# First group of a fused cross-attention and FFN kernel, rebuilt: load order, Wq centred first, angle sums on GpSimd, real part of four tiles before the imaginary part

## The chip, the cores and the metric

One core of one Trainium2 chip runs the whole program. The metric is the time of an execution on the device in microseconds (us). The core's engines are TensorE (PE in the profile, PEld for its weight loads), VectorE (DVE), ScalarE (ACT), GpSimd (POOL) and SyncE (SP), which issues nearly all transfers. They run side by side and meet only at semaphores.

## The reference

```python
x = x + xattn(layernorm(x), ctx_1024, mask, Wq, bq, Wk, bk, Wv, bv, Wo, bo)   # x: (2, 2048, 512), ctx: (2, 77, 512)
#   Q = q @ Wq + bq; K = ctx @ Wk + bk; V = ctx @ Wv + bv        one head, 77 keys
#   softmax(where(mask, Q K^T / sqrt(512), -1e9)) V @ Wo + bo
h = layernorm(x)
real = h @ cos(theta + theta_noise)                              # theta, phi: (512, 512)
imag = h @ sin(phi + phi_noise)
x = x + sqrt(real * real + imag * imag)
```

## The kernel before

The 4096 rows of x are cut into eight groups of 512 rows, four tiles of 128 rows each; groups alternate between the two batches. Each engine has its own program, written out by hand in the order in which it is to run, and semaphores join them.

**Prepared once.** K is made from the context and Wk, then `A = Wq K^T` (one 512 x 154 matrix for both batches), so that the scores of a group are `x^T` chunks times `A`, and a row `c = bq K^T`. A is centred over its rows (the layer norm's mean is taken out that way): ScalarE copies A to `a_raw`, TensorE multiplies it with `ones_mean`, VectorE subtracts. V times Wo gives `vw`, 77 rows for each batch. The angle matrices come in halves of 128 x 1024. For each half: the sum with the noise (`sum_angle`; theta on VectorE, phi on GpSimd), `turns_of` on ScalarE (two passes that round to whole turns), `reduce_angle` on VectorE (lines 714, 717, 720), `sine` on ScalarE (lines 566, 568: the sine and its fp16 high part `w_hi`), and `low_half_of_sine` on VectorE (line 726: the rest, `w_lo`, counted by `w_ready`: 2 is all of cos, 4 is all of sin).

**Each group.** `scores` on TensorE; `softmax_shift` on VectorE, `exps` on ScalarE, `softmax_total` on VectorE; `attend` on TensorE; `residual` on VectorE (line 793, with the statistics of the second layer norm, 796 and 803); `rstd_of_x2` on GpSimd (341 to 348); `high_half` on ScalarE (591, 596) and `low_half` on VectorE (807), which split the normed rows into two fp16 halves; a DMA transposition of each tile (`transpose_h`, SP line 256); `feed(n, j, part)`, twelve fp16 matmuls of 512 columns for tile j and part 0 (real) or 1 (imaginary); `square` on ScalarE, `add_squares` on VectorE, `roots`, `finish` and the store.

**The first group (0)** attends in fp32 with `vw` itself. All later groups use `vw` scaled by its largest entry and split into fp16 halves, stacked in `vw_stack`. The largest entry is found so: `key_max` on VectorE, a transposition on TensorE, `vw_max` on VectorE, a matmul that spreads it over the partitions, four small VectorE operations up to `vw_scale`; then ScalarE scales and rounds (`vw_hi_ready`), the low half is taken (`vw_lo_ready`), SP stacks both by three transfers. Only with these, and with the probabilities of group 1 split (`high_probs`, `low_probs`) and transposed by a DMA (`transpose_probs(1)`), can `attend(1, 1, 0)` run.

TensorE's program from the first `feed` on: eight feeds of group 0, with the four `attend(1, 1, j)` and `scores(2, 0)` between them, then `step(1)`, whose first is `feed(1, 0, 0)`, up to `step(6)` and the last group. `x_loaded[b]` counts the loads of a batch's x buffer `xb[b]`, `stats_of_x(b, blk)` waits for it; `load_x(0, 1)` brings the rows of group 2 into the buffer that group 0 used.

## Time and profile before

| | |
|---|---|
| time, median of 3 runs | 267.83 us (267.27 to 268.71) |
| span of the profiled execution, first to last instruction | 265.4 us |
| time of the profiled execution itself | not given; 267.8 - 265.4 = 2.4 us lie around the span |
| TensorE busy | 240.6 us (91%) |
| VectorE, ScalarE, GpSimd busy | 183.0, 148.8, 65.7 us |
| matmuls of the first group start | 50.0 us |
| matmuls of the second group start | 86.4 us |
| mean granted clock of TensorE | 0.976 |

An engine's busy share is a mean over the whole run. The run has two stages with different limits: up to 86.4 us the preparation and the first group, in which every engine waits for others at some places, and from there a steady stage. The change is in the first.

### The profile page before, as it was taken

Reading aid. Unit: us, or ns where it says so; the run is one execution under the profiler, and the core shown is the slowest. Engines: PE = TensorE matmul, PEld = TensorE weight load, DVE = VectorE, ACT = ScalarE, POOL = GpSimd, SP = SyncE. Lnnn points to the kernel's source line nnn. Section 1 sums busy time; section 2 is a strip of 40 time slices with the busy share of each in tenths; the row PEclk is TensorE's granted clock in tenths of the full one; section 3 lists DMA queues with packets and bytes.
Section 4 is the critical chain, followed back from the end, with each engine's and each line's share of the span. In section 5 each row is a group of like instructions: output and inputs, shape, how many; then the busy total and the mean of one; then the engine's idle time right before and its main releaser. Section 6 shows DMA issues by size and latency. Waiting matters only on the chain.

```text
span 265.4 us, 3879 instructions
## 1 busy us (share of the span) xinstructions
PE 240.6 (91%) x1223; PEld 132.0 (50%) x1223; DVE 183.0 (69%) x348; ACT 148.8 (56%) x203; POOL 65.7 (25%) x158
## 2 busy tenths in 40 slices
PE   0989779859966999999999999999999999999991
PEld 0899334524722444744474456445644654444440
DVE  2038799995886787778787777786768662964442
ACT  0248477655705792676378447745773577266341
POOL 1000646571334203310430233024203310132000
PEclk9999958999979999999999999999999999999998
DMA  6999930458122895396359736862695244324531
GB/s 210 388 424 411 416 127 0 63 187 229 42 45 40 189 220 227 61 252 206 161 99 244 270 90 169 175 277 59 187 211 235 42 80 79 161 40 79 198 116 46
DMA packets 47948, 44.79 MB, mean 169 GB/s; under 512 B 42454, under 2 KB 42454, under 8 KB 44605
## 3 DMA queue, kind: packets, MB, share of 16 engines
q1 hardware_dynamic: 47269, 44.42, 55.5%
q10 hardware_dynamic: 664, 0.18, 0.3%
q8 instruction: 8, 0.13, 0.2%
q14 instruction: 7, 0.06, 0.1%
HBM read 25.66 MB, written 8.39 MB: 128 GB/s over the span
## 4 chain that ended last, share of the span: by engine, by line
PE 72%; DVE 14%; DMA 4%; POOL 4%; issue 3%; ACT 2%; SPq 0%; DVEq 0%; POOLq 0%; ACTq 0%
PE re L445 10%; PE re L446 10%; PE re L447 10%; PE im L445 9%; PE im L446 9%; PE im L447 9%; PE score_bank L416 7%; DVE angle_w L714 2%; PE att L432 2%; PE att L434 2%; DVE angle_w L717 2%; DMA wk<-in_Wk 2%; DVE stats L735 2%; DVE x L793 1%; DVE stats L796 1%
## 5 line engine op out<-in xcount | busy, mean ns | idle before, releaser
L445 PE MATMUL re<-w_hi,hT 128*128 128x512 f16 x128 | 49.0, 383 | 4.2 <-DMA hT<-h_split 4.2
L591 ACT ACTIVATE h<-x,shift,rstd 128x512 f32<-128x512 f32 x32 | 26.0, 813 | 42.9 <-POOL shift L348 42.9
L445 PE MATMUL im<-w_hi,hT 128*128 128x512 f16 x128 | 48.5, 379 | 0.8 <-DVE w_lo L726 0.8
L446 PE MATMUL re<-w_lo,hT 128*128 128x512 f16 x128 | 49.0, 383 | 0.0
L447 PE MATMUL re<-w_hi,hT 128*128 128x512 f16 x128 | 48.9, 382 | 0.0
L447 PE MATMUL im<-w_hi,hT 128*128 128x512 f16 x128 | 48.5, 379 | 0.0
L446 PE MATMUL im<-w_lo,hT 128*128 128x512 f16 x128 | 48.5, 379 | 0.0
L807 DVE SCALAR_TENSOR_TENSOR h_split<-h,h_split 128x512 f16<-128x512 f32 x32 | 22.0, 689 | 21.2 <-ACT h_split L596 21.2
L416 PEld LDWEIGHTS score_bank<-a_keys,xTb 128*128 128x128 f32 x256 | 29.8, 192 | 1.3 <-issue 0.5
L341 POOL TENSOR_TENSOR veps<-mv,eps 128x1 f32<-128x1 f32 x32 | 11.6, 362 | 73.4 <-DVE mv L803 73.4
L416 PE MATMUL score_bank<-a_keys,xTb 128*128 128x77 f32 x256 | 29.5, 274 | 0.0
L334 POOL TENSOR_TENSOR veps<-mv,eps 128x4 f32<-128x4 f32 x8 | 4.5, 557 | 95.9 <-DVE mv L741 95.9
L602 ACT ACTIVATE sq_re<-re 128x512 f32<-128x512 f32 x32 | 18.6, 583 | 15.2 <-PE re L447 10.3
L824 DVE TENSOR_TENSOR wv<-x,wk 128x2048 f32<-128x2048 f32 x7 | 16.0, 2292 | 15.0 <-ACT wk L607 12.3
L816 DVE TENSOR_TENSOR wk<-sq_re,sq_im 128x512 f32<-128x512 f32 x32 | 21.9, 684 | 5.3 <-ACT sq_im L602 3.8
L793 DVE SCALAR_TENSOR_TENSOR x<-att,inv_total,xb 128x512 f32<-128x512 f32 x32 | 23.6, 736 | 2.1 <-PE att L434 1.9
L602 ACT ACTIVATE sq_im<-im 128x512 f32<-128x512 f32 x32 | 18.8, 588 | 10.1 <-PE im L447 10.1
L796 DVE BATCH_NORM_STATS2 stats<-x 128x6 f32<-128x512 f32 x32 | 22.2, 694 | 1.1
L445 PEld LDWEIGHTS re<-w_hi,hT 128*128 128x128 f16 x128 | 12.7, 99 | 20.6 <-ACT sq_re L602 2.6
L596 ACT ACTIVATE h_split<-h 128x512 f16<-128x512 f32 x32 | 20.2, 632 | 1.5
L445 PEld LDWEIGHTS im<-w_hi,hT 128*128 128x128 f16 x128 | 12.7, 100 | 15.3 <-DVE w_lo L726 0.8
L447 PEld LDWEIGHTS re<-w_hi,hT 128*128 128x128 f16 x128 | 12.6, 98 | 15.5 <-issue 0.6
(115 smaller groups left out, 333.6 us busy)
## 6 DMA issues: line engine op xcount, KB each, us to landing
xTb<-in_xT SPq DMA_DIRECT2D x8, 1024.0 KB, 5.0
xb<-in_x SPq DMA_DIRECT2D x8, 1024.0 KB, 5.5
out_rows<-wv SPq DMA_DIRECT2D x7, 1024.0 KB, 3.9
wk<-in_Wk SPq DMA_DIRECT2D x2, 512.0 KB, 5.3
wqT<-in_WqT SPq DMA_DIRECT2D x1, 1024.0 KB, 8.3
angle_w<-in_theta SPq DMA_DIRECT2D x2, 512.0 KB, 10.2
angle_n<-in_theta_noise SPq DMA_DIRECT2D x2, 512.0 KB, 10.9
wv<-in_Wv SPq DMA_DIRECT2D x1, 1024.0 KB, 13.5
```

The source lines that it names most:

```text
L416: last = nc.tensor.matmul(score_bank[:, KEYS * j:KEYS * j + KEYS], xTb[:, k, P * j:P * j + P], a_keys[:, k, KEYS * batch:KEYS * batch + KEYS],
L445: nc.tensor.matmul(bank_[:, :], hT[j][:, 0, k, :], w_hi[part][:, k, :], start=(k == 0), stop=False)
L446: nc.tensor.matmul(bank_[:, :], hT[j][:, 0, k, :], w_lo[part][:, k, :], start=False, stop=False)
L447: last = nc.tensor.matmul(bank_[:, :], hT[j][:, 1, k, :], w_hi[part][:, k, :], start=False, stop=(k == CH - 1))
L591: nc.scalar.activation(h[j % 2][:, :], x2[b][:, j, :], ACT.Identity, bias=shift2[:, j:j + 1], scale=rstd2[:, j:j + 1]).then_inc(h_made, 1)
L596: nc.scalar.activation(h_split[j][:, 0, :], h[j % 2][:, :], ACT.Copy, scale=H_SCALE).then_inc(hi_made, 1)
L602: nc.scalar.activation((sq_re, sq_im)[part][j % 2][:, :], (re_bank, im_bank)[part][j % 2][:, :], ACT.Square, scale=UNSCALE).then_inc((re_s ...
L793: nc.vector.scalar_tensor_tensor(out=x2[b][:, j, :], in0=att_bank[j % 2][:, :], scalar=inv_total[:, j:j + 1], in1=xb[b][:, j, :], op0=ALU. ...
L796: nc.vector.bn_stats(stats2[:, j, :], x2[b][:, j, :]).then_inc(stats2_made, 1)
L807: nc.vector.scalar_tensor_tensor(out=h_split[j][:, 1, :], in0=h[j % 2][:, :], scalar=H_SCALE, in1=h_split[j][:, 0, :], op0=ALU.mult, op1=A ...
L816: nc.vector.tensor_tensor(power[:, j, :], sq_re[j % 2][:, :], sq_im[j % 2][:, :], ALU.add).then_inc(power_made, 1)
L824: nc.vector.tensor_tensor(result[:, :, :], x2[b][:, :, :], power[:, :, :], ALU.add).then_inc(result_made, 1)
```

## The change

1. **Loads.** `WqT` comes in four chunks, then `xT` and `x` of group 0, `Wv`, the first half of theta, `Wo`, the other half, phi. Before: `WqT` whole, theta, `Wv`, `xT`, `x`, `Wo`, phi. The load of group 1's x goes behind the first two transpositions, and `load_x(0, 1)` from before the third transposition to behind `transpose_probs(1)`.
2. **A.** VectorE centres the rows of Wq itself, chunk by chunk (`bn_stats`, `bn_aggr`, subtract), before the product; `a_raw`, `a_mid` and the mean matmul go; `a_keys` is made from PSUM by VectorE with scale and mask in one pass.
3. **TensorE.** Eleven matmuls on zeros at the very start; `scores(0, 0)` ahead of the V products; the real part of four tiles, then the imaginary part of four tiles, each tile with a PSUM bank of its own (`feed_first`); `scores(2, 0)` goes behind the attends.
4. **Angles.** All four sums on GpSimd; the quarter turn of the cosine is put into the bias of ScalarE's sine, with the absolute value taken by a bitwise VectorE pass instead of the clamp. `sine(1, 1)` stands behind the scaling of `vw`.
5. **`vw`.** `key_max` takes the absolute value itself; ScalarE makes the high half in one pass; the low half goes from GpSimd to VectorE, behind `low_half_of_sine(1, 1)`.
6. ScalarE loads the exp table at the start and the sine table by a dummy; `step(1)` and `step(2)` of ScalarE and steps 1 to 4 of VectorE are written out instead of looped.

```diff
             for half in range(2):
                 chunks = slice(CH // 2 * half, CH // 2 * half + CH // 2)
                 sp.dma_start(wk[:, chunks, :], Wk[:, chunks, :]).then_inc(ld_wk[half], 16)
-            sp.dma_start(wqT[:, :, :], WqT).then_inc(ld_wq, 16)
-            load_angles(0, 0)
-            load_angles(0, 1)
-            sp.dma_start(wv[:, :, :], Wv).then_inc(ld_wv, 16)
+            for k in range(CH):
+                sp.dma_start(wqT[:, k, :], WqT[:, k, :]).then_inc(ld_wq[k], 16)
             load_xT(0, 0)
             load_x(0, 0)
+            sp.dma_start(wv[:, :, :], Wv).then_inc(ld_wv, 16)
+            load_angles(0, 0)
             sp.dma_start(wo[:, :, :], Wo).then_inc(ld_wo, 16)
+            load_angles(0, 1)
             load_angles(1, 0)
             load_angles(1, 1)
-            load_x(1, 0)
...
             transpose_h(0, [0, 1])
-            sp.wait_ge(x2_made, TILES)
-            load_x(0, 1)
+            load_x(1, 0)
             transpose_h(0, [2])
...
             transpose_probs(1)
+            sp.wait_ge(x2_made, TILES)
+            load_x(0, 1)
             transpose_h(1, [0, 1])
...
             rstd_of_x(0)
-            sum_angle(0)
-            sum_angle(1)
-            for j in range(TILES):
-                rstd_of_x2(0, j)
+            sum_angle(0, 0)
+            sum_angle(0, 1)
+            sum_angle(1, 0)
+            rstd_of_x2(0, 0)
+            rstd_of_x2(0, 1)
+            sum_angle(1, 1)
+            rstd_of_x2(0, 2)
+            rstd_of_x2(0, 3)
             rstd_of_x(1)
-            pool.wait_ge(vw_hi_ready, 1)
-            nc.gpsimd.tensor_tensor(vw_lo[:, :, :], vw_scaled[:, :, :], vw_stack[0][0:KEYS, :, :],
-                                    ALU.subtract).then_inc(vw_lo_ready, 1)
...
+            pe.wait_ge(warm_made, 1)
+            for _ in range(WARM):
+                nc.tensor.matmul(prep[7][:, :], warm[:, 0:P], warm[:, :], start=True, stop=True)
...
+            pe.wait_ge(vw_ready, 2)
             pe.wait_ge(w_ready, 2)
-            feed(0, 0, 0)
-            feed(0, 1, 0)
+            feed_first(0, 0)
+            feed_first(1, 0)
+            feed_first(2, 0)
 
             pe.wait_ge(key_max_made, 1)
             nc.tensor.transpose(pT_bank[0:1, 0:KEYS], key_max[:, :], ident[0:KEYS, 0:KEYS]).then_inc(key_max_mm, 1)
+            feed_first(3, 0)
             pe.wait_ge(vw_max_made, 1)
             nc.tensor.matmul(pT_bank[:, P:P + 1], ones_row[:, :], vw_max[:, :], start=True, stop=True).then_inc(vw_max_mm, 1)
             pe.wait_ge(w_ready, 4)
-            feed(0, 0, 1)
-            feed(0, 1, 1)
-            feed(0, 2, 0)
-            feed(0, 2, 1)
-            scores(2, 0)
+            feed_first(0, 1)
+            feed_first(1, 1)
             pe.wait_ge(vw_stacked, 3 * 16)
             attend(1, 1, 0)
-            feed(0, 3, 0)
             attend(1, 1, 1)
+            feed_first(2, 1)
             attend(1, 1, 2)
-            feed(0, 3, 1)
             attend(1, 1, 3)
+            scores(2, 0)
+            feed_first(3, 1)
...
             exps(0)
+            turns_of(0, 0)
             act.wait_ge(pT_mm, 1)
             nc.scalar.activation(probsT[:, :], pT_bank[0:KEYS, :], ACT.Copy).then_inc(pT_copied, 1)
+            nc.scalar.activation(act_scratch[:, 1:2], zero[:, :], ACT.Sin)
+            act.wait_ge(half_pi_made, 1)
+            sine(0, 0)
+            turns_of(0, 1)
+            high_half(0, 0, 0)
+            high_half(0, 0, 1)
+            sine(0, 1)
             turns_of(1, 0)
...
+            high_half(0, 0, 2)
+            high_half(0, 0, 3)
+            sine(1, 0)
             turns_of(1, 1)
+            square_first(0, 0)
+            square_first(1, 0)
+            act.wait_ge(vw_scale_made, 2)
+            nc.scalar.activation(vw_stack[0][0:KEYS, :, :], vw[:, :, :], ACT.Copy,
+                                 scale=vw_scale[0:KEYS, 0:1]).then_inc(vw_hi_ready, 1)
             sine(1, 1)
+            square_first(2, 0)
+            square_first(3, 0)
             exps(1)
             high_probs(1)
+            square_first(0, 1)
+            square_first(1, 1)
...
+            for k in range(CH):
+                dve.wait_ge(ld_wq[k], 16)
+                nc.vector.bn_stats(wq_stats[:, k, :], wqT[:, k, :]).then_inc(wq_stats_made, 1)
+                dve.wait_ge(wq_stats_made, k + 1)
+                nc.vector.bn_aggr(wq_mean[:, k, :], wq_stats[:, k, :]).then_inc(wq_mean_made, 1)
+                dve.wait_ge(wq_mean_made, k + 1)
+                nc.vector.tensor_scalar(wqT[:, k, :], wqT[:, k, :], wq_mean[:, k, 0:1], None,
+                                        ALU.subtract).then_inc(wq_centred, 1)
```

VectorE's order after the keys (each name is a function above; `values_ready(b)` adds `bo` to `vw`):

```
softmax_shift(0), softmax_total(0), reduce_angle(0,0), values_ready(0), residual(0,0), residual(0,1),
low_half_of_sine(0,0), reduce_angle(0,1), low_half(0,0), residual(0,2), low_half(0,1), values_ready(1),
residual(0,3), low_half_of_sine(0,1), reduce_angle(1,0), key_max, low_half(0,2), low_half(0,3),
low_half_of_sine(1,0), reduce_angle(1,1), vw_max, stats_of_x(1,0), vw_scale, softmax_shift(1),
low_half_of_sine(1,1), vw_lo, low_probs(1), softmax_total(1), add_squares(0,0), stats_of_x(0,1),
mean_of_x(2), residual(1,0), add_squares(0,1), residual(1,1), low_half(1,0), ...
```

## Rows read from the trace of the kernel before

**Rows 1.** The page: GB/s in the 40 slices of 6.6 us.

```profile
GB/s 210 388 424 411 416 127 0 63 187 229 42 45 40 189 220 227 61 252 206 161 99 244 270 90 169 175 277 59 187 211 235 42 80 79 161 40 79 198 116 46
```

**Rows 2.** Windows: stretch, its length, busy us by engine, granted clock, DMA.

```profile
73.50:75.50 2.00, 0.00 (x1) 0.00 (x0) 2.00 (x5) 0.00 (x0) 0.00 (x0) 0.97 0.69 134
75.50:78.70 3.20, 3.12 (x8) 1.17 (x9) 2.95 (x9) 0.00 (x0) 1.51 (x3) 0.50 0.00 0
...
86.30:265.40 179.10, 173.32 (x880) 88.41 (x880) 122.95 (x242) 104.73 (x144) 34.92 (x111) 0.99 0.55 154
```

**Rows 3.** Timeline of TensorE: start us, us, engine line op out<-in [idle before <-releaser].

```profile
49.99 0.38 PE L445 MATMUL re<-w_hi,hT 128*128 128x512 f16 x1 [0.72 <-DMA hT<-h_split]
...
69.81 3.69 PE L416 MATMUL score_bank<-a_keys,xTb 128*128 128x77 f32 x32
75.58 0.59 PE L432 MATMUL att<-vw_stack,pT 128*128 128x512 f16 x1 [2.07 <-issue]
...
86.36 0.39 PE L445 MATMUL re<-w_hi,hT 128*128 128x512 f16 x1 [2.14 <-DMA hT<-h_split]
```

**Rows 4.** Loads: SyncE's and VectorE's timeline, DMA issues (us to landing).

```profile
6.31 0.50 SPq L243 DMA_DIRECT2D wo<-in_Wo  x1
...
15.92 1.23 DVE L704 SCALAR_TENSOR_TENSOR angle_w<-angle_w,angle_n 128x1024 f32<-128x1024 f32 x1 [1.33 <-DMA angle_n<-in_theta_noise]
...
wo<-in_Wo SPq DMA_DIRECT2D x1, 1024.0 KB, 20.5
```

**Rows 5.** Timeline from the statistics of x to the first softmax.

```profile
28.15 0.38 DVE L741 BATCH_NORM_AGGREGATE mv<-stats 128x2 f32<-128x6 f32 x4
28.61 1.28 POOL L334 TENSOR_TENSOR veps<-mv,eps 128x4 f32<-128x4 f32 x1 [26.77 <-DVE mv L741]
...
31.12 0.92 DVE L751 SCALAR_TENSOR_TENSOR logits<-score_bank,rstd,c_keys 128x77 f32<-128x77 f32 x4 [1.29 <-POOL rstd L336]
```

**Rows 6.** Timeline of GpSimd's angle sums and VectorE beside them.

```profile
30.97 4.89 POOL L328 TENSOR_TENSOR angle_w<-angle_w,angle_n 128x1024 f32<-128x1024 f32 x2
...
32.58 1.07 DVE L760 TENSOR_TENSOR shifted<-logits,top 128x308 f32<-128x308 f32 x1
...
34.18 2.76 DVE L714 SCALAR_TENSOR_TENSOR angle_w<-turns,angle_w 128x1024 f32<-128x1024 f32 x1
...
90.11 0.48 DVE L760 TENSOR_TENSOR shifted<-logits,top 128x308 f32<-128x308 f32 x1
```

**Rows 7.** Groups by line, 0 to 75 us: busy us, mean ns, idle before.

```profile
L735 DVE BATCH_NORM_STATS2 stats<-xb 128x6 f32<-128x512 f32 x11 | 6.8, 680 | 0.0
...
L717 DVE SCALAR_TENSOR_TENSOR angle_w<-turns,angle_w 128x1024 f32<-128x1024 f32 x4 | 4.9, 1228 | 0.1
...
L726 DVE SCALAR_TENSOR_TENSOR w_lo<-angle_n,w_hi 128x1024 f16<-128x1024 f32 x4 | 4.8, 1210 | 0.1
...
L793 DVE SCALAR_TENSOR_TENSOR x<-att,inv_total,xb 128x512 f32<-128x512 f32 x4 | 3.0, 746 | 0.1
...
L720 DVE TENSOR_SCALAR angle_w<-angle_w 128x1024 f32<-128x1024 f32 x4 | 2.8, 694 | 0.1
```

**Rows 8.** Timeline: tile 3 of group 0, from its statistics to ScalarE.

```profile
55.10 0.18 DVE L803 BATCH_NORM_AGGREGATE mv<-stats 128x2 f32<-128x6 f32 x1
...
60.37 0.81 ACT L591 ACTIVATE h<-x,shift,rstd 128x512 f32<-128x512 f32 x1 [2.71 <-POOL shift L348]
```

**Rows 9.** Timeline of ScalarE: a table load and what follows it.

```profile
25.13 1.28 ACT L566 ACT_TABLE_LOAD   x1
...
26.43 1.06 ACT L566 ACTIVATE angle_n<-angle_w 128x1024 f32<-128x1024 f32 x1
```

**Rows 10.** SyncE's timeline and DMA issues of short windows (us to landing).

```profile
72.33 1.27 SPq L263 DMA_TRANSPOSE pT<-p_split  x1
...
hT<-h_split SPq DMA_TRANSPOSE x1, 3.1
...
xb<-in_x SPq DMA_DIRECT2D x1, 1024.0 KB, 5.8
```

More of the change, by code:

```diff
@@ L401, in _ @@
             last.then_inc(c_mm, 1)
-            pe.wait_ge(a_copied, CH)
-            for k in range(CH):
-                last = nc.tensor.matmul(prep[1][:, 0:KK], ones_mean[:, :], a_raw[:, k, :],
-                                        start=(k == 0), stop=(k == CH - 1))
-            last.then_inc(mean_mm, 1)
             def scores(m, batch):
@@ L480, in _ @@
             attend_first(1)
[L481 removed]
+            project_values(1, range(1, CH))
             attend_first(2)
@@ L607, in roots @@
                 nc.scalar.activation(power[:, :, :], power[:, :, :], ACT.Sqrt).then_inc(root_made, 1)
[L609 to L613 removed]
             act.wait_ge(ld_bv, 16)
             for c in range(CH):
[L616 removed]
+                bank_ = prep[2 + c] if c < 2 else prep[4 + c]
                 act.wait_ge(vT_mm, c + 1)
```

246 lines of the change are left out of this document (132 added, 114 removed).

## The prediction

> **What bounds the kernel now.** I read the slices and windows first. From 86.3 us on TensorE is busy 173.3 of 179.1 us, the rest being the tail in which the last group is stored, and the clock is full [rows 2]. No other engine can lengthen that stage and nothing in it is left to gain. So the span is the moment at which `feed(1, 0, 0)` starts, 86.4 us [rows 3], plus 179.0 us, and the change, which alters no work behind that point, is worth what it does to that moment; call it T1. The chain of waits says the same: before T1 it runs through loads, VectorE, GpSimd and ScalarE in turn, behind it through TensorE alone. TensorE's timeline gives the marks: the first feed (F0) at 50.0, T1 at 86.4, hence 36.4 us between for eight feeds, four attends and `scores(2, 0)`. A feed is twelve matmuls at 0.215 us, 2.6 us; the scores are 3.7 [rows 3]; an attend 0.43. That is 26.2 us of work and 10.2 of waits, among them 2.1 before the attends and 2.1 before T1, and a stretch at 1.2 GHz (granted clock 0.50) of 3.2 us after TensorE had idled for 2.0 us [rows 2], 1.6 us lost. I build the new T1 in four legs, each from rows.
>
> **Leg 1, loads and keys.** Data arrives at 1024 KB in 2.7 us: the second half of theta, 4.3 such units into the order, releases VectorE at 15.9, and Wo, at 8.3 units, lands at 6.3 + 20.5 = 26.8 [rows 4]; the slices from 6.6 to 33 us, 388 to 424 GB/s, show no slack [rows 1]. By this rate the new order brings WqT at 10.5, xT 13.2, x 15.9, Wv 18.6, theta 21.3 and 26.8, Wo 24.0, phi 29.5 and 32.2. Three more issues on SyncE lie under the transfers. VectorE centres a chunk of Wq in 0.68 (statistics) + 0.18 + 0.35 (half of line 720, 0.69) and gaps, 1.3 us [rows 7, 8]; four from 8.5 on end at 13.7. The keys then need a last quarter product, the c product and five short VectorE passes; I say 16.8, and it can't beat x at 15.9. Statistics of x take 2.5 us (four, overlapping), so 19.3, and from there to the logits it was 31.1 - 28.2 = 3.0 us [rows 5]: 22.3. That is 8.8 us before today's 31.1. The eleven zero matmuls and the early exp table gain nothing more here, since VectorE's centring ends last.
>
> **Leg 2, up to F0.** Here the gain is spent. GpSimd now sums all four halves. Two of them took 4.9 us; within it VectorE's `shifted` took 1.07 where it takes 0.48 later, and line 714 took 2.76 against 1.2 of its neighbour 717 [rows 6, 7]. So a sum is some 2.2 us, and a VectorE pass with two SBUF inputs stands still until the sum ends. (The Trainium skill, "SBUF — State Buffer", section "Who interferes with whom", says that such a pass and a GpSimd operation that reads SBUF exclude each other for the whole instruction, whoever starts first. The trace agrees, with 1.5 us of wait. By it each sum can cost its whole length, and F0 would be the upper bound below, 52.8, where a sharing of the port would leave 48.4.)
>
> The first softmax ends its shift at 22.3 + 2.5 = 24.8 with one lock in it, as before; exp 25.3; `turns_of(0, 0)`, two passes of 1.06 [rows 9], at 27.6. But the second sum can't start before theta lands, 26.8, and holds VectorE until 29.0. From there VectorE's list up to `low_half_of_sine(0, 1)`: two `reduce_angle` at 3.2, two low halves of sines at 1.2, four residuals at 1.65 (0.75 + 0.68 + 0.18 and gaps), two `low_half` and two `values_ready` at 0.7, and 1.2 of waiting for the first attend: 19.4 us [rows 7]. (Passes that have no row are taken by width: 512 columns 0.7, 1024 columns 1.2 on VectorE, 1.1 on ScalarE, narrower ones 0.2 to 0.5.) F0 = 48.4 if nothing more holds it. Two more sums, phi's, are asked for in the middle of `reduce_angle` passes that wait for each other; each can slip into a gap and cost 2.2. Bounds 48.4 and 52.8; I take one of the two, 50.6. Behind these GpSimd operations stand `rstd_of_x2`, and behind them `high_half` on ScalarE; they fit beside the list. F0 thus stays where it is: `reduce_angle(0, 0)` and its sine, which stood ahead of the softmax, now stand behind it (4.4 us), and a lock, the late theta half and the attend's wait eat the rest.
>
> **Leg 3, from F0 to the end of sine(1, 1) (S).** The real feeds need no such thing, but `sine(1, 1)` now waits on ScalarE for the scale of `vw`, and every imaginary feed waits for it. VectorE up to the scale: two `reduce_angle` 6.4, key_max 1.2, two `low_half` 1.4, low sine 1.2, vw_max 0.2, statistics 2.5 + 0.4, small ones 0.6: 13.9. Then ScalarE, high half 1.2 and the two sine passes 2.1. That is 17.2 without any wait. Waits: tile 3 took 5.3 us from its statistics to ScalarE [rows 8], which makes `low_half(0, 3)` 0.5 late; `sine(1, 0)` stands behind it on ScalarE, 1.4; the turns behind that, 0.9: 20.1 at most. I take the middle, 18.7: S = 69.3, and the imaginary feeds start at 70.6. TensorE has finished the real ones by 63 to 65 and idles 5 us or more; if its clock falls, 1.6 us [rows 2], that hides in leg 4, where TensorE alone would be done 6.9 early.
>
> **Leg 4, from S to T1.** TensorE alone would need 1.3 + 10.4 (four feeds) + 1.7 + 3.7 = 17.1. It isn't alone. SyncE issues `load_x(0, 1)` only behind `transpose_probs(1)`, VectorE's `stats_of_x(0, 1)` waits for that load, and `residual(1, 1, 0)` stands behind it; `attend(1, 1, 2)` and `attend(1, 1, 3)` need the first and the second residual for their banks, and the scores and the last feed stand behind the attends. Added up: two squares 1.2; exp table 1.3 and exp 0.5; `high_probs` 0.7; `low_probs` 0.5; issue of the transposition 1.3 [rows 10]; the load 5.8 behind a transposition [rows 10], 4.7 at least; statistics 2.5 + 0.4; residual 0.75 with statistics 0.9; add 0.7; residual 0.75; attend 0.45; scores 3.7; feed 2.6. Sum 24.0, bounds 22.9 and, if the idle before the third attend drops the clock once more [rows 2], 25.6. The second group's own way (statistics, GpSimd, ScalarE, transposition 3.1 [rows 10]) ends some 2 us before T1 and is covered. (The Trainium skill, "ScalarE: Activation LUTs", "What ACT_TABLE_LOAD costs", gives a switch 1.28 us and a drain of 1.38. Here the next pass starts 1.3 us after the load began [rows 9], so the trace shows the first figure alone; by the page this leg would be 1.4 longer.)
>
> Removed work that gains nothing: the mean product, `a_raw`, the second pass over `vw`, two table loads and GpSimd's `vw_lo`, for they lie in the legs where something else ends last, or are already left out of the sums. Written-out steps change nothing behind T1, where TensorE is never short.
>
> **The sum.** T1 = 50.6 + 18.7 + 24.0 = 93.3, 6.9 later than 86.4. Span 265.4 + 6.9 = 272.3. The median is 2.4 above the profiled span; the same 2.4 gives 274.7 us. Bounds: 48.4 + 17.2 + 22.9 = 88.5, which is 269.9; 52.8 + 20.1 + 25.6 = 98.5, which is 279.9.
>
> **Rivals.** *A, packed VectorE (faster).* VectorE is the engine that sets F0. If the sums never hold it and the turns are always ready, its list starts at 24.3 rather than 29.0 and has no attend wait: 24.3 + 0.6 + 18.2 = F0 43.1. With leg 3 and 4 as taken T1 is 85.8, with the shortest 83.2: 267.2 to 264.6, 265.9 in the middle. It decides from F0 below 43.7, or below 46.3 with the shortest legs. For it: nothing but VectorE's own list and the locks stands between. Against: theta lands at 26.8, and the locks are seen [rows 6]. 13 in 100.
> *B, the load is hidden anyway (no change).* If x(0, 1) is there when VectorE asks, leg 4 is TensorE's 17.1 and T1 = 86.4: 267.8 us. For it: leg 4's late end rests on one transfer. Against: the load is issued behind a wait for `low_probs(1)`, and VectorE asks for it within 2 us. 9 in 100.
> *C, locks and clock at their worst.* Both phi sums hold VectorE and the clock drops twice: 279.9, nearly 280. For it: tile 3's way over GpSimd took 5.3 us beside VectorE's passes [rows 8], for a few tiny operations. 13 in 100.
> *The forecast* as above, 65 in 100, its own range 270 to 278.
>
> **Numbers.** Differences under 0.5% (1.3 us) can't be told from none. Faster: A, and what of B falls there, 15 in 100. Within 0.5%: 10. Slower: the forecast and C, 75. For 8 in 10 the range must reach into B from below and stop short of C's end: 267.0 to 279.5.
>
> **What would show it.** Right: the first logits at 22 to 23; VectorE passes of lines 714 or 717 of over 2 us beside GpSimd's sums; the first feed at 48 to 53; TensorE idle for at least 5 us between the real and the imaginary feeds, released by `w_lo`; `stats_of_x(0, 1)` released by the DMA of x; `feed(1, 0, 0)` at 88 to 98, and from there the same 179 us. Wrong: a first feed before 46; imaginary feeds that start before 64, which would mean that the scale of `vw` came early; an x load that nobody waits for; or new waits of TensorE behind T1, which would break the 179.

## The result, and the profile after

The changed kernel takes 282.97 us (median of 4 runs, 282.16 to 283.65) beside 267.55 for the kernel before (267.26 to 268.71): ratio 1.055, 95% interval 1.050 to 1.060. It is slower. The measured time lies 8.3 us above the 274.7 predicted, and above the range's upper end of 279.5. The profiled execution took 283.65 us with a span of 281.9.

The page of the changed kernel (busy us; granted clock and GB/s in 40 slices of 7.05 us; the chain that ended last; a group with its idle time before):

```profile
span 281.9 us, 3842 instructions
...
PE 252.4 (90%) x1226; PEld 135.1 (48%) x1226; DVE 190.2 (67%) x361; ACT 143.0 (51%) x196; POOL 61.8 (22%) x160
...
PEclk9999859797779589999999999999999999999997
...
GB/s 203 392 412 405 298 0 1 223 123 102 22 183 26 41 216 164 216 64 237 187 151 98 247 246 79 199 234 165 48 249 187 151 80 106 90 100 74 186 85 66
...
PE 75%; DVE 11%; DMA 6%; ACT 4%; issue 2%; SPq 1%; DVEq 0%
...
L459 PE MATMUL re<-w_hi,hT 128*128 128x512 f16 x128 | 50.2, 393 | 9.6 <-DVE w_lo L763 9.6
```

TensorE is busy 11.8 us longer than before. Some 3 of that are the zero matmuls at the start (249.3 us in the run without them, below); the rest is put down to the same work at a lower clock (slices 5 to 15), which was not added up. The 9.6 us of idle time ahead of the feeds, released by `w_lo`, are the two places at which TensorE waits for sines. The loads run at 392 to 412 GB/s in slices 2 to 4, as before [rows 1].

Windows of the changed kernel (columns as in [rows 2]):

```profile
53.50:57.50 4.00, 3.92 (x11) 1.51 (x12) 3.93 (x4) 1.45 (x3) 2.28 (x4) 0.57 0.57 231
71.30:76.40 5.10, 0.00 (x0) 0.00 (x0) 3.52 (x12) 4.37 (x6) 0.00 (x0) 0.77 0.10 31
87.40:92.00 4.60, 0.97 (x4) 0.27 (x4) 4.46 (x12) 0.00 (x0) 2.61 (x6) 0.90 0.00 0
92.00:99.50 7.50, 7.50 (x35) 7.22 (x34) 4.65 (x10) 3.37 (x5) 2.21 (x7) 0.50 0.20 38
102.80:281.90 179.10, 173.37 (x881) 88.40 (x879) 119.96 (x236) 102.34 (x141) 33.23 (x106) 0.99 0.53 151
```

For TensorE the last row is the row of before [rows 2] over again: 179.1 us with 173.4 of work. So all of the difference in span, 281.9 - 265.4 = 16.5 us, was made before the second group's feeds, as the prediction's frame says. TensorE's timeline gives the marks (columns as in [rows 3]):

```profile
35.46 3.78 PE L429 MATMUL att<-vw,probsT 77*128 77x512 f32 x4 [4.71 <-DVE vw L883]
...
53.58 0.59 PE L459 MATMUL re<-w_hi,hT 128*128 128x512 f16 x1 [4.43 <-DVE w_lo L763]
...
61.52 0.39 PE L459 MATMUL im<-w_hi,hT 128*128 128x512 f16 x1 [0.95 <-DMA hT<-h_split]
...
66.54 0.39 PE L459 MATMUL im<-w_hi,hT 128*128 128x512 f16 x1 [2.18 <-DMA hT<-h_split]
...
76.47 0.61 PE L459 MATMUL re<-w_hi,hT 128*128 128x512 f16 x1 [5.17 <-DVE w_lo L763]
...
89.46 0.38 PE L436 MATMUL att<-vw_stack,pT 128*128 128x512 f16 x1 [2.03 <-DVE x L832]
...
91.66 0.58 PE L436 MATMUL att<-vw_stack,pT 128*128 128x512 f16 x1 [1.60 <-DVE x L832]
```

A first duration of 0.58 to 0.61 us where it is otherwise 0.38 or 0.39 is a matmul at 1.2 GHz: the window from 53.50 on has a granted clock of 0.57, the one from 92.00 on 0.50. The legs of the prediction, read off the timelines:

| leg | ends at | measured | predicted (bounds) |
|---|---|---|---|
| 1, first logits | 22.09 | 22.1 | 22.3 |
| up to the first feed (F0) | 53.58 | 53.6 | 50.6 (48.4 to 52.8) |
| 3, F0 to the end of `sine(1, 1)` | 75.16 | 21.6 | 18.7 (17.2 to 20.1) |
| 4, from there to T1, `feed(1, 0, 0)` | 102.85 | 27.7 | 24.0 (22.9 to 25.6) |

Three excesses of 3.0, 2.9 and 3.7 make the 9.6 us by which the span was missed (272.3 forecast). Where the prediction assumed 2.4 us between span and median, there are 1.1 here (282.97 - 281.9), which leaves the 8.3. These 1.3 are no work that went away. In every execution on record the time is 1.7 to 1.9 us above that execution's span. The profiled execution before was about 0.6 faster than the median, the one after 0.7 slower.

**Where leg 2 went.** Timeline of the changed kernel, GpSimd's sums and the VectorE passes beside them:

```profile
27.37 2.35 POOL L333 TENSOR_TENSOR angle_w<-angle_w,angle_n 128x1024 f32<-128x1024 f32 x1 [2.52 <-DMA angle_n<-in_theta_noise]
...
27.75 3.05 DVE L746 SCALAR_TENSOR_TENSOR angle_w<-turns,angle_w 128x1024 f32<-128x1024 f32 x1 [1.35 <-ACT turns L579]
...
30.12 2.88 POOL L333 TENSOR_TENSOR angle_w<-angle_w,angle_n 128x1024 f32<-128x1024 f32 x1 [0.41 <-DMA angle_n<-in_phi_noise]
...
30.84 3.25 DVE L749 SCALAR_TENSOR_TENSOR angle_w<-turns,angle_w 128x1024 f32<-128x1024 f32 x1
...
37.57 0.75 DVE L832 SCALAR_TENSOR_TENSOR x<-att,inv_total,xb 128x512 f32<-128x512 f32 x1 [2.17 <-PE att L429]
...
43.25 1.23 DVE L749 SCALAR_TENSOR_TENSOR angle_w<-turns,angle_w 128x1024 f32<-128x1024 f32 x1
...
44.49 2.35 POOL L333 TENSOR_TENSOR angle_w<-angle_w,angle_n 128x1024 f32<-128x1024 f32 x1
...
44.52 2.87 DVE L754 TENSOR_SCALAR angle_w<-angle_w 128x1024 int32<-128x1024 int32 x1
```

Each VectorE pass beside a sum ends about one pass behind the sum's end: 29.72 and 30.80, 33.00 and 34.09, 46.84 and 47.39. That fits a pass that stands still until the sum ends, not one that runs slower. The lock works both ways: the sum at 30.12 began while a pass ran until 30.80, and took 2.88 us instead of 2.35. The third pass is the bitwise pass, which has only one input and takes 0.69 us where nobody disturbs it (at 34.11). (The Trainium skill, "SBUF — State Buffer", "Who interferes with whom", names both kinds, a pass with two SBUF inputs and a `tensor_scalar` in a two-port mode, as shut out while GpSimd's instruction holds the shared port. The trace agrees in the durations, 3.25 for 1.23 and 2.87 for 0.69; in which mode the bitwise pass ran it does not show.)

**Where legs 3 and 4 went.** From the chain of waits of the changed kernel (start, us, what):

```profile
58.42 1.23 SPq L260
59.70 0.57 SPq L229
60.38 6.11 DMA hT<-h_split
...
71.98 1.15 ACT vw_stack L668
...
76.15 1.28 ACT L600
...
80.61 5.17 DMA xb<-in_x
85.80 2.48 DVE stats L772 x4
...
92.67 6.74 PE score_bank L420 x32
```

and the timeline of VectorE and ScalarE at the two joints:

```profile
71.33 0.16 DVE L925 TENSOR_SCALAR vw_max_all<-pT_bank 128x1 f32<-128x1 f32 x1 [3.60 <-PE pT_bank L530]
...
71.98 1.15 ACT L668 ACTIVATE vw_stack<-vw,vw_scale 77x1024 f16<-77x1024 f32 x1 [9.44 <-DVE total_scale L930]
...
85.80 2.47 DVE L772 BATCH_NORM_STATS2 stats<-xb 128x6 f32<-128x512 f32 x4 [2.99 <-DMA xb<-in_x]
```

ScalarE is idle for 9.44 us until it gets the scale of `vw`. VectorE, which makes that scale, in turn waits 3.60 for TensorE, which is still in the real feeds. The transposition issued at 60.4, 0.7 us behind the load of xT, took 6.1 us; the one of [rows 10] took 3.1. The load of x(0, 1) arrives 3.0 us after VectorE asks, the third and fourth attends wait for the residuals, and the scores behind them run at 1.2 GHz: 6.74 us where they take 3.69 in [rows 3].

### The profile page after: what moved, and what is told of

It is laid out like the page before. It is cut to its first block, busy times and chain, and to the rows that moved or that the text cites. A ratio compares the mean times of both kernels' runs of the same rounds, so it can differ in the third digit from the quotient of the medians.

```text
span 281.9 us, 3842 instructions
## 1 busy us (share of the span) xinstructions
PE 252.4 (90%) x1226; PEld 135.1 (48%) x1226; DVE 190.2 (67%) x361; ACT 143.0 (51%) x196; POOL 61.8 (22%) x160
## 4 chain that ended last, share of the span: by engine, by line
PE 75%; DVE 11%; DMA 6%; ACT 4%; issue 2%; SPq 1%; DVEq 0%
PE score_bank L420 10%; PE im L459 10%; PE im L460 10%; PE im L461 9%; PE re L459 9%; PE re L460 9%; PE re L461 9%; DMA hT<-h_split 2%; PE att L436 2%; DVE angle_w L749 2%; PE att L438 2%; DVE angle_w L746 2%; DMA xb<-in_x 2%; DMA wk<-in_Wk 2%; PE att L429 1%
## 5 line engine op out<-in xcount | busy, mean ns | idle before, releaser
L459 PE MATMUL re<-w_hi,hT 128*128 128x512 f16 x128 | 50.2, 393 | 9.6 <-DVE w_lo L763 9.6
L459 PE MATMUL im<-w_hi,hT 128*128 128x512 f16 x128 | 49.8, 389 | 3.1 <-DMA hT<-h_split 3.1
L461 PE MATMUL re<-w_hi,hT 128*128 128x512 f16 x128 | 49.8, 389 | 0.0
L461 PE MATMUL im<-w_hi,hT 128*128 128x512 f16 x128 | 49.3, 385 | 0.0
L420 PEld LDWEIGHTS score_bank<-a_keys,xTb 128*128 128x128 f32 x256 | 33.1, 210 | 1.6 <-issue 0.8
L420 PE MATMUL score_bank<-a_keys,xTb 128*128 128x77 f32 x256 | 32.8, 291 | 0.0
L346 POOL TENSOR_TENSOR veps<-mv,eps 128x1 f32<-128x1 f32 x32 | 9.3, 290 | 74.0 <-DVE mv L842 74.0
L459 PEld LDWEIGHTS re<-w_hi,hT 128*128 128x128 f16 x128 | 12.8, 100 | 25.6 <-issue 6.2
L636 ACT ACTIVATE sq_im<-im 128x512 f32<-128x512 f32 x28 | 16.5, 588 | 16.0 <-PE im L461 16.0
L636 ACT ACTIVATE sq_re<-re 128x512 f32<-128x512 f32 x28 | 16.3, 583 | 15.1 <-PE re L461 15.1
L860 DVE TENSOR_TENSOR wk<-sq_re,sq_im 128x512 f32<-128x512 f32 x28 | 19.2, 685 | 4.5 <-ACT sq_im L636 3.8
L772 DVE BATCH_NORM_STATS2 stats<-xb 128x6 f32<-128x512 f32 x32 | 19.7, 678 | 3.0 <-DMA xb<-in_x 3.0
## 6 DMA issues: line engine op xcount, KB each, us to landing
angle_w<-in_theta SPq DMA_DIRECT2D x2, 512.0 KB, 15.8
angle_n<-in_theta_noise SPq DMA_DIRECT2D x2, 512.0 KB, 17.2
```

The lines of the kernel that those rows point to most:

```text
L420: last = nc.tensor.matmul(score_bank[:, KEYS * j:KEYS * j + KEYS], xTb[:, k, P * j:P * j + P], a_keys[:, k, KEYS * batch:KEYS * batch + KEYS],
L459: nc.tensor.matmul(bank_[:, :], hT[j][:, 0, k, :], w_hi[part][:, k, :], start=(k == 0), stop=False)
L461: last = nc.tensor.matmul(bank_[:, :], hT[j][:, 1, k, :], w_hi[part][:, k, :], start=False, stop=(k == CH - 1))
L636: nc.scalar.activation((sq_re, sq_im)[part][j % 2][:, :], (re_bank, im_bank)[part][j % 2][:, :], ACT.Square, scale=UNSCALE).then_inc((re_s ...
L772: last = nc.vector.bn_stats(stats1[:, j, :], xb[b][:, j, :])
L860: nc.vector.tensor_tensor(power[:, j, :], sq_re[j % 2][:, :], sq_im[j % 2][:, :], ALU.add).then_inc(power_made, 1)
```

## The experiments

Differences are between medians; every ratio is to the kernel before, run beside it (267.4 to 268.4 us), with its 95% interval. A timeline shows one execution of a kernel, and some of its marks differ from one execution to the next; where that matters it is said.

**One part undone at a time, from the changed kernel.**

*The load of x(0, 1) back to where it was:*

```diff
             load_x(1, 0)
+            sp.wait_ge(x2_made, TILES)
+            load_x(0, 1)
             transpose_h(0, [2])
...
             transpose_probs(1)
-            sp.wait_ge(x2_made, TILES)
-            load_x(0, 1)
```

> The changed kernel (T1, the first feed of group 1, at 102.9 us; median 283.0), with the load of group 2's x issued right behind the load of group 1's x instead of behind the transposition of the probabilities. Theory (the late x load holds two residuals, and the idle of TensorE that comes of it throws the clock down to 1.2 GHz for 9.4 us): VectorE's statistics start with no wait at some 83, the third attend no longer waits, the scores take 3.7 and not 6.9 us; T1 at 94 to 96, the time 275 to 276. Rival 1 (the load holds two residuals but the low clock has another cause): T1 only 3 us earlier, 280. Rival 2 (the load is covered by TensorE's work): no change, 283.

275.45 us, ratio 1.026 (1.017 to 1.036): 7.5 less than the changed kernel. TensorE's timeline of this run, the last attend, which had waited 1.60 us, and the scores behind it:

```profile
87.39 0.38 PE L436 MATMUL att<-vw_stack,pT 128*128 128x512 f16 x1 [0.72 <-DVE x L832]
...
87.82 3.69 PE L420 MATMUL score_bank<-a_keys,xTb 128*128 128x77 f32 x32
```

The statistics no longer wait, and the scores take 3.69 instead of 6.74. T1 93.94, 8.9 earlier. The move of one load is the largest single cost that was undone here. Of the 8.9, 1.3 were there before leg 4: the fourth real feed ran at full clock in this execution, behind a wait of 2.29 us, and the imaginary feeds started at 75.13 instead of 76.47.

*The last sine ahead of the scaling of `vw`:*

```diff
+            sine(1, 1)
             act.wait_ge(vw_scale_made, 2)
             nc.scalar.activation(vw_stack[0][0:KEYS, :, :], ...)
-            sine(1, 1)
...
             mean_of_x(1)
+            low_half_of_sine(1, 1)
```

> The changed kernel with the last sine ahead of the scaling of vw on ScalarE, and its low half on VectorE ahead of the scale too. Theory (the 5.2 us that TensorE idles between real and imaginary feeds are the chain scale, high half, sine, low half): the imaginary feeds start right behind the real ones, at 71.3 instead of 76.5, and find the full clock; but the high half, the exp of group 1 and so the attends move only by the 2.1 us of the sine, and the late x load by as much: T1 2 to 3 us earlier, the time 280 to 281. Rival (the imaginary feeds are on the path to the end): T1 5 to 7 us earlier, 276 to 278.

279.49 us, 1.041 (1.033 to 1.049): 3.5 less, which lies between the theory's range and the rival's. The imaginary feeds start at 69.10 instead of 76.47, 7.4 earlier, T1 only 4.6: the x load is now waited for longer (5.16 us, 2.99 before this edit), and that takes the rest back. TensorE's and then VectorE's timeline of this run:

```profile
78.39 0.38 PE L436 MATMUL att<-vw_stack,pT 128*128 128x512 f16 x1 [3.94 <-issue]
```

```profile
81.60 2.47 DVE L772 BATCH_NORM_STATS2 stats<-xb 128x6 f32<-128x512 f32 x4 [5.16 <-DMA xb<-in_x]
```

*Phi's sums left out:*

```diff
-                nc.gpsimd.tensor_tensor(angle_w[part][:, cols_], ..., angle_n[part][:, cols_], ALU.add)
+                if part == 1: nc.gpsimd.memset(spare[:, :], 0.0)
+                else:         nc.gpsimd.tensor_tensor(...)
```

> The changed kernel with the two sums of phi and its noise left out (a one-column memset in their place, so the noise of phi is missing from the output). Theory (a GpSimd sum stops a VectorE pass with two SBUF inputs): line 749 from 3.25 back to 1.2 us, line 754 from 2.9 to 0.7, the first feed at 49 to 50 instead of 53.6, T1 some 4 us earlier, the time 278.5 to 279.5. Rival 1 (those two passes are long for another reason): all marks as they are, 283. Rival 2 (something else holds the first feed, the high halves on ScalarE or the transpositions): passes short, first feed less than 2 us earlier.

277.66 us, 1.033 (1.025 to 1.041): 5.3 less, a little more than expected; F0 48.15, which is 5.4 earlier. The passes are back at 1.23 and 0.69 us. That gives the 2.0 and 2.2 of standing still. VectorE also waits less for the first attend, 1.22 instead of 2.17, since the first four attends take 2.08 instead of 3.78. This last part does not belong to the sums. In two other runs it goes the other way, fast attends with the sums and slow ones without them (TensorE's timelines, first of the next run, then of the rebuilt order without phi's sums further below):

```profile
35.04 2.29 PE L429 MATMUL att<-vw,probsT 77*128 77x512 f32 x4 [3.75 <-DVE vw L894]
```

```profile
32.93 3.68 PE L432 MATMUL att<-vw,probsT 77*128 77x512 f32 x4 [1.91 <-DVE vw L886]
```

The length of the idle time ahead of them does not decide it: 3.75 us here were followed by fast attends, 1.91 by slow ones.

*Zero matmuls at five places where TensorE waits, so that it keeps its clock* (`idle_work(b, n)` is n matmuls on zeros into bank b)*:*

```diff
+            idle_work(3, 20)
             pe.wait_ge(vw_ready, 2)
             pe.wait_ge(w_ready, 2)
...
+            idle_work(3, 8)
             feed_first(3, 0)
...
+            pe.wait_ge(re_squared, 1)
+            idle_work(0, 20)
             pe.wait_ge(w_ready, 4)
...
+            pe.wait_ge(re_squared, 4)
+            idle_work(3, 9)
             attend(1, 1, 2)
+            idle_work(3, 7)
             attend(1, 1, 3)
```

> The changed kernel with matmuls on zeros in TensorE's idle places: 20 before the first feed, 8 before the fourth, 20 before the imaginary feeds, 9 and 7 before the last two attends of group 1. They write banks that are overwritten later. Theory (the clock falls because TensorE idles, and the stretches at 1.2 GHz cost 1.6 us after the first feed, 1.8 in the fourth, 1.5 in the imaginary feeds and 4.7 at the scores): granted clock 1.0 in all of them; the fourth real feed ends 2 to 4 us earlier, the scores take 3.7; together T1 6 to 8 us earlier, the time 275 to 277. Rival (only the last stretch is on the path, the others hide behind the x load): 278 to 279. Rival 2 (the filling delays the real work as much as the clock gives): 282 to 284.

278.53 us, 1.039 (1.030 to 1.047): 4.4 less (5.8 by the spans of the profiled executions), not the 6 to 8 expected but in the first rival's range; mean clock 0.987 instead of 0.934. T1 comes 6.6 earlier: 1.5 up to F0, 0.7 up to the imaginary feeds, 4.5 behind their start, where the scores are back at 3.69. The 1.5 are not the edit's: they stand in the fast first attends and in theta's held pass, both before the first added matmul at 46.4. What is left is 5.1 at T1, most of it in leg 4, of which 0.8 is lost again behind T1, where the stage takes 179.9. So the added matmuls are worth 4 to 5 us. With the clock restored VectorE waits 5.27 us for x(0, 1), so part of what they give runs into the x load.

*No zero matmuls at the start:*

```diff
-WARM = 11
+WARM = 0
```

> The changed kernel without the eleven matmuls on zeros at the start. Theory (VectorE's centring ends last in leg 1, and the keys' product follows it chunk by chunk): the Wk products run at 1.2 GHz and end some 2 us later, at 12.6, so that the four quarter products and c follow each other without waits and end at 17.9 or so instead of 16.9; logits later by up to 1 us, and nothing of it left at T1 beyond that: 283 to 284. Rival (the warm start is worth its full 2 us at the end): 285.

283.35 us, 1.055 (1.048 to 1.062), no difference. The logits come 1.85 us later (23.94, where up to 1 us was expected), yet VectorE's line 749 starts at 30.86, in the changed kernel at 30.84. VectorE's timeline of this run:

```profile
23.94 0.91 DVE L790 SCALAR_TENSOR_TENSOR logits<-score_bank,rstd,c_keys 128x77 f32<-128x77 f32 x4 [1.50 <-issue]
```

That is the clearest sign of what the early softmax is worth: the late half of theta, with GpSimd's sum behind it, sets this place.

*Theta ahead of Wv and Wo:*

```diff
-            sp.dma_start(wv[:, :, :], Wv).then_inc(ld_wv, 16)
             load_angles(0, 0)
-            sp.dma_start(wo[:, :, :], Wo).then_inc(ld_wo, 16)
             load_angles(0, 1)
+            sp.dma_start(wv[:, :, :], Wv).then_inc(ld_wv, 16)
+            sp.dma_start(wo[:, :, :], Wo).then_inc(ld_wo, 16)
```

> The changed kernel with both halves of theta loaded ahead of Wv and Wo. Theory (the first logits are 9 us early but VectorE's reduce_angle waits for theta's second half, which lands at 27.3, is summed on GpSimd until 29.7, and holds line 746 at 3 us; so the early softmax buys nothing): theta's sums end by 27.5, line 746 runs in 1.2 us from 28 on, line 749 starts 1 to 2 us earlier, the V products and vw come later but in time; first feed at 51.5 to 52.5 instead of 53.6, T1 1 to 2 us earlier, the time 281 to 282. Rival 1 (the load order costs nothing here): first feed at 53.6, 283. Rival 2 (vw now comes last: Wo lands at 26.8, attends at 34 or later and the same end): line 749 earlier, first feed not.

284.77 us, 1.059 (1.053 to 1.065): the theory fell. VectorE's timeline of this run:

```profile
31.57 0.47 DVE L808 TENSOR_REDUCE total<-probs 128x4 f32<-128x308 f32 x1 [7.28 <-ACT probs L600]
...
33.61 1.23 DVE L746 SCALAR_TENSOR_TENSOR angle_w<-turns,angle_w 128x1024 f32<-128x1024 f32 x1 [1.35 <-ACT turns L579]
34.87 1.22 DVE L749 SCALAR_TENSOR_TENSOR angle_w<-turns,angle_w 128x1024 f32<-128x1024 f32 x1
```

The first exp stands on ScalarE behind the copies of V out of PSUM, so a late Wv holds it 7.3 us. The reductions start 5.9 us later, but undisturbed, VectorE waits 1.22 instead of 2.17 for the first attend, and F0 (54.54) is only 1.0 later.

**The undone parts together, and what was left then.**

*The first two edits, and with them:*

```diff
-            transpose_h(0, [2])
+            transpose_h(0, [2, 3])
             sp.wait_ge(scores_mm, 2)
             load_xT(0, 1)
-            transpose_h(0, [3])
```

> The changed kernel with three things moved: group 2's x load early, the last sine ahead of the scale of vw, and the load of group 2's xT behind the fourth transposition. Theory (leg 3 and leg 4 each have one late item, and the transposition beside the xT load took 6.1 us instead of 3.1): fourth real feed from 64.5 and not 66.5, imaginary feeds at 69 to 70, attends at 78 to 80, T1 at 88 to 91, the time 268 to 271. Rival (each removed wait is replaced by another of the same length in the chain of the second group: softmax, split, transposition): T1 no better than with the x load alone, 94 to 96, 275.

272.32 us, 1.016 (1.010 to 1.023), 1.3 above the upper end expected. The fourth real feed starts 10.8 us after F0 instead of 13.0: the four transpositions now take 3.0 to 3.2 us each. With the x load alone moved, the fourth still took 6.2. T1 91.74, again with 179.1 us behind it.

*To that:*

```diff
             feed_first(1, 1)
+            scores(2, 0)
             pe.wait_ge(vw_stacked, 3 * 16)
...
             attend(1, 1, 3)
-            scores(2, 0)
```

> The kernel with three things moved (272.3 us, T1 at 91.7), and scores(2, 0) ahead of the attends of group 1 again, where TensorE idles 4.4 us. Theory (T1 then hangs on attend(1,1,0), at 78.6, by residual, statistics, GpSimd, the two ScalarE passes, low half and transposition, 9.8 us in the kernel before): T1 at 88.5 to 89.5, the time 269.5 to 270.5. Rival (TensorE's order still sets T1): 85.6 to 87, the time 267 to 268.

271.00 us, 1.010 (1.007 to 1.013), 0.5 above the range expected. T1 comes 3.5 earlier (88.27), the time only 1.3. What is lost lies behind T1: TensorE's first 4 us there have a granted clock of 0.59, and the stage takes 180.7 us instead of 179.1.

*The same with theta ahead of Wv (diff as above):*

> The former kernel with theta loaded ahead of Wv as well. Theory: what the load order gives at the first feed (1 to 2 us) comes through to T1, for the chain from VectorE's list over the scale of vw to the attends has no slack: 268 to 269.5. Rival (the fourth transposition and the scale of vw absorb it): as the former kernel.

271.90 us, 1.014 (1.009 to 1.019), no gain where 1.5 to 3 us were expected; F0 is 1.1 later (54.48), as in the run of theta alone.

*The rebuilt order with the scores ahead, and phi's sums moved from GpSimd to VectorE (`sum_phi` is the same addition):*

```diff
-            sum_angle(1, 0)
...
-            sum_angle(1, 1)
...
             values_ready(0)
+            sum_phi(0)
...
             values_ready(1)
+            sum_phi(1)
```

> The kernel with three things moved and the scores forward (271.0 us; first feed at 53.4, T1 at 88.3), and both sums of phi on VectorE, one where it waits for the first attend, one behind values_ready(1). Theory (each GpSimd sum costs VectorE 2.0 to 2.2 us, one on VectorE itself costs 1.2, and the first of them lies in a wait of 2.2 us): line 749 in 1.2 and line 754 in 0.7 us, first feed at 50.3, 3 us earlier, and all of it at T1: 267.5 to 268.5. Rival (the sum on VectorE costs what it saves): 271.

267.01 us, 0.995 (0.992 to 0.998), 4.0 less than with GpSimd's sums and a little better than expected. VectorE does 2.4 us of additional work (two passes of 1.21) and F0 is 3.8 earlier all the same (49.52). The first attends were fast in this execution (2.24 us; 3.78 in the one it is compared with), so not all of the 3.8 need be the sums'.

*The same order with phi's sums left out instead (diff as in the first run of that kind):*

> The same kernel with the two phi sums on GpSimd left out (the noise of phi is missing from the output). Theory (the cost of the locks and the cost of the late items add up, for they lie one behind the other): first feed at 48 to 49, T1 at 83 to 84, the time 265.5 to 266.5, 5 us less than with them, as in the changed kernel. Rival (they overlap): 268 to 270.

267.15 us, 0.996 (0.992 to 1.000): to leave phi's noise out altogether is worth no more than to sum it on VectorE. The saving (3.9) is smaller than the 5.3 in the changed kernel, and the time lies between the theory's range and the rival's. So whether the costs add up is not settled. In the profiled execution F0 is at 48.77, as expected, but the first attends are slow (3.68 us, shown above) and the third real feed has a granted clock of 0.60, so that T1 (85.29) comes later than with VectorE's sums (84.40).

*Phi's sums on VectorE, and theta's second one too:*

```diff
-            sum_angle(0, 1)
...
             softmax_total(0)
+            sum_theta_1()
```

> The rebuilt order with both halves' phi sums on VectorE (the run before it of that kind took 267.0 us, first feed at 49.5), and theta's second half summed on VectorE too, behind softmax_total(0). Theory (GpSimd's sum beside VectorE is what made the first reduction 3.0 us): the reduction goes back to 1.2 us and the sum costs VectorE 1.2 us, so VectorE's list gets some 0.5 to 1.5 us shorter: first feed at 48.0 to 49.0, time 265.5 to 266.5. Rival (theta's landing at 27.3 us, and not the lock, sets this leg): the sum waits for the landing, the reduction of the second half starts where it did, first feed at 49.3 to 49.8, time 267.

266.01 us, 0.990 (0.987 to 0.993). VectorE's timeline, first of the run with phi's sums alone on VectorE, where GpSimd's sum of theta runs beside the pass, then of this one:

```profile
27.84 3.02 DVE L750 SCALAR_TENSOR_TENSOR angle_w<-turns,angle_w 128x1024 f32<-128x1024 f32 x1 [1.35 <-ACT turns L576]
```

```profile
27.85 1.23 DVE L740 TENSOR_TENSOR angle_w<-angle_w,angle_n 128x1024 f32<-128x1024 f32 x1 [1.35 <-DMA angle_n<-in_theta_noise]
28.99 1.22 DVE L756 SCALAR_TENSOR_TENSOR angle_w<-turns,angle_w 128x1024 f32<-128x1024 f32 x1
```

The interval just meets that of the run before, and in the two profiled executions the spans are equal (264.4 us), since the clock behind T1 is low in this one and full in the other. What can be read is the place itself. The sum and the first pass together end at 30.2 instead of 30.9, and F0 is 0.64 earlier (48.88), in the theory's range and out of the rival's. Of the 1.8 us for which the pass was held only a third was to be had; the rest is the time of the sum itself, which now stands on VectorE.

**The kernel before, with small parts of the change.** All three start from it.

```diff
+            for _ in range(WARM):
+                nc.tensor.matmul(prep[7][:, :], warm[:, 0:P], warm[:, :], start=True, stop=True)
...
+            nc.scalar.activation(act_scratch[:, 0:1], zero[:, :], ACT.Exp)
```

> The kernel before, with only two parts of the change: eleven matmuls on zeros at the start and the exp table loaded by a dummy. Theory (in the kernel before the keys hang on TensorE and on the table load, 1.3 + 1.9 us, and VectorE is full from 20.5 us on): first keys 2.8 us earlier, VectorE's list up to the first feed 1 to 2.5 us earlier (x lands at 23.4 and bounds it), T1 by as much: the time 265.5 to 266.5. Rival (the x load and GpSimd's sums eat it): 267.5, no change.

266.24 us, 0.993 (0.991 to 0.996), as expected: 1.2 less than the kernel before, measured beside it. The first feed is 1.1 earlier (48.84), T1 2.2 (84.11).

*The change's way with `vw` added:*

```diff
-            nc.scalar.activation(vw_scaled[:, :, :], vw[:, :, :], ACT.Abs).then_inc(vw_abs_made, 1)
...
-            nc.gpsimd.tensor_tensor(vw_lo[:, :, :], vw_scaled[:, :, :], vw_stack[0][0:KEYS, :, :], ALU.subtract)
...
             softmax_shift(1, 1)
-            add_squares(0, 0)
+            nc.vector.scalar_tensor_tensor(out=vw_lo[:, :, :], in0=vw[:, :, :], scalar=vw_scale[0:KEYS, 0:1], ...)
             low_probs(1)
+            add_squares(0, 0)
```

> The kernel before with the zero matmuls, the early exp table, and the change's way with vw: the absolute value in key_max, the high half in one pass of ScalarE, the low half on VectorE. Theory: attends of group 1 wait for exp, split and transposition; one pass of 1.1 us less ahead of the exp and no GpSimd operation beside VectorE's shift (2.2 us where it takes 0.5) bring the attends 1 to 2.5 us forward beyond the former kernel, T1 hangs on attend(1,1,0) by the second group's chain of 9.8 us: 264 to 265. Rival (TensorE's own work, not the attends, sets T1 then): same as the former.

264.88 us, 0.988 (0.983 to 0.993), the fastest version found. Its interval overlaps that of the run before, so that the second step helps by itself is likely and not settled. In the profiled execution (266.17 us, slower than the median) the attends behind the scores start at 1.2 GHz:

```profile
74.50 0.58 PE L435 MATMUL att<-vw_stack,pT 128*128 128x512 f16 x1 [2.01 <-issue]
```

*Zero matmuls in that gap:*

```diff
             scores(2, 0)
+            pe.wait_ge(re_squared, 2)
+            for _ in range(9):
+                nc.tensor.matmul(re_bank[1][:, :], warm[:, 0:P], warm[:, :], start=True, stop=True)
             pe.wait_ge(vw_stacked, 3 * 16)
```

> The kernel before with early table, zero matmuls and the new way with vw (264.9 us), and nine matmuls on zeros between scores(2, 0) and the attends, where TensorE idled 2.0 us and then ran 3.2 us at 1.2 GHz. Theory (that stretch delays the later attends and with them residuals and the second group's transpositions): granted clock 1.0 there, T1 at 84 to 85 instead of 85.3, the time 263.5 to 264.5, and less spread between runs. Rival (T1 hangs on the first attend alone, which the clock touches by 0.3 us): 264.9, no change.

266.52 us, 0.992 (0.989 to 0.995), no faster than without them: the theory fell. The windows of this run say why (columns as in [rows 2]):

```profile
75.40:79.50 4.10, 4.10 (x21) 1.85 (x19) 2.59 (x5) 0.00 (x0) 1.40 (x4) 1.00 0.02 4
...
85.00:89.00 4.00, 3.96 (x12) 1.53 (x13) 3.82 (x10) 2.73 (x3) 1.54 (x4) 0.64 0.62 115
```

The clock was kept, at 1.00, but the attends start 1.0 us later, and TensorE then waits for the second group's transposition anyway (2.49 us; 2.17 without the zeros). T1 is nearly the same (85.04; 85.33 without), and now the clock drops behind it, where nothing hides it: 0.64, and the stage takes 180.8 us instead of 179.1.

## Why the prediction was right or wrong

**Right in the changed kernel, not in every run: the frame.** The span is T1 + 179. It holds in the changed kernel (281.9 - 102.85 = 179.05) and, within 0.1, in seven of the runs. In the other eight the stage takes 179.9 to 180.8. Four of them have a granted clock of 0.57 to 0.64 in the first 4 us behind T1. The other four (x load early, zero matmuls in the waits, phi's sums on VectorE, phi's sums left out of the rebuilt order) keep the full clock, and TensorE waits there instead: the first attend behind T1 starts 11.1 to 11.5 us after it, where it is 10.4 in the changed kernel and in the run with three things moved. TensorE's timeline with phi's sums on VectorE:

```profile
95.54 0.39 PE L433 MATMUL att<-vw_stack,pT 128*128 128x512 f16 x1 [0.39 <-DMA pT<-p_split]
```

That is the sign that the prediction had named as breaking the 179, new waits of TensorE behind T1.

**Leg 1: its gain is spent, as forecast; its number is right by luck.** Logits at 22.1. 9.0 us were gained there, and F0 is 3.6 later than before; the run without zero matmuls shows that logits 1.85 us later cost nothing, since theta's second half lands only at 27.3. VectorE's timeline of the changed kernel:

```profile
17.71 2.47 DVE L772 BATCH_NORM_STATS2 stats<-xb 128x6 f32<-128x512 f32 x4
...
22.09 0.92 DVE L790 SCALAR_TENSOR_TENSOR logits<-score_bank,rstd,c_keys 128x77 f32<-128x77 f32 x4 [1.50 <-issue]
```

The statistics ended 0.9 later than the 19.3 taken, and from there to the logits it was 1.9 us instead of 3.0 (GpSimd's first operation took 0.20 us instead of the 1.28 of [rows 5]). The two misses cancel. That the zero matmuls "gain nothing more here" was wrong for the leg: without them the logits are 1.85 later, and VectorE waits 2.99 us for the keys' product.

**Wrong in size: leg 2, "I take one of the two".** Both of phi's sums held VectorE, for 2.0 and 2.2 us, 4.2 together where 2.2 was taken. The first attend cost 2.17 of waiting instead of 1.2, with the four attends at a low clock (3.78 us); in three runs in which they took 1.98 to 2.29 it cost 1.22, as forecast. Theta's held pass ended at 30.8, 0.6 later than taken. Together 3.6 more, against 3.0 measured: the rest of the list took 0.6 less. The upper bound of 52.8 held both sums, but no price for the clock.

**Wrong in size: leg 3, the list of VectorE as the only bound.** The mechanism that was named, ScalarE in wait for the scale of `vw`, is there (9.44 us). But VectorE itself waited 3.60 for TensorE. Without that it would have ended F0 + 18.0, inside the bounds. (The terms of the upper bound add up to 20.0, not 20.1.) TensorE took 17.7 us from F0 to the spread of the maximum: 10.4 for four feeds, 3.1 waiting for transpositions, and most of the other 4.2 from stretches at 1.2 GHz (granted clock 0.57 in the first four). The prediction had said that TensorE has finished by 63 to 65; it did so at 71, 3.0 of it because F0 was late. Two terms are missing, and other runs give the size of each by the time from F0 to the start of that spread. With the fourth feed at full clock, and the transposition still 6.2 us long, it was 15.8 instead of 17.3 (the x load early): 1.5 for the clock. With the last sine moved it was 15.5, and 13.4 when the load of xT also stood behind the fourth transposition: 2.0 for the transposition beside a load (6.1 us for 3.1).

**Wrong in size: leg 4, "if the idle before the third attend drops the clock once more".** The wait for x(0, 1) was right, down to its length (5.2 us of load for 5.8 taken). The clock drop was left out of the value and had 1.6 us in the bound. It came, and it covered the last attend, all of the scores and the first five matmuls of the last feed: 0.4 + 3.0 + 1.0 = 4.4 us more. Against that the load had landed 0.7 earlier than the sum has it. The price 1.6 came from a row in which 3.2 us ran slow [rows 2]; here 7.5 us and more did (the window from 92.0). The run with zero matmuls confirms the size: 4.5 us of T1. The wait and the drop belong together: with x(0, 1) loaded early, the scores take 3.69 us too.

**The rivals.** Packed VectorE needed that no sum held VectorE; theta's sum held it until 30.8. The load was not hidden. The third, locks and clock at their worst, given 13 in 100, came nearest with 279.9: both sums did hold VectorE. Even it was 3 too low, for each leg went past its upper bound, by 0.8, 1.5 and 2.1 us.

**Where the time went, in sum.** From the changed kernel 10.7 us come back with the x load, the last sine and the xT load moved, 1.3 with the scores, 4.0 with phi's sums on VectorE, 1.0 with theta's: 17.0 in all, more than the whole loss. So the rest of the change (Wq centred first, the new load order, real parts before imaginary ones) costs nothing that these runs show; but freed of these costs it reaches 266.0, and the old order with the small edits reaches 264.9 to 266.2. No run here separates these two. In leg 3 the share of the clock and that of the transposition come from comparing profiled executions, one for each kernel, and are no better known than that.

## What to carry to other kernels

A load may be moved to a later place of an in-order queue only after asking what each wait ahead of it waits for: here it landed behind probabilities, was 3 us late, and cost 7.5. Price a wait of TensorE by the work that stands behind it until the engine is back at full clock, not by the gap alone; but fill such a gap only if nothing later would be waited for anyway. An addition on GpSimd is not free work beside VectorE: the sum of a half took 2.35 us and held VectorE for 2.0 to 2.2, where VectorE does it in 1.21.
